# A three-layer macaron block on one core: each quad's maxima split on VectorE, side products in column tiles, another order of the plan

## The reference

```python
def ffn(x, W1, b1, W2, b2):
    h = relu(einsum('bsd,fd->bsf', x, quantize(W1)) + b1)      # 128 -> 512
    return einsum('bsf,df->bsd', h, quantize(W2)) + b2         # 512 -> 128
def attn(x, ...):                                              # 16 heads of 8
    q, k, v = (x @ W.T + b split into heads for W, b in ...)
    q, k = rope(q, k)
    scores = einsum('bhnd,bhmd->bhnm', q, k) / sqrt(8)
    return (softmax(scores) @ v).reshape(B, N, 128) @ Wo.T + bo
x = x + 0.5 * ffn(layernorm(x))
x = x + attn(layernorm(x))
x = x + 0.5 * ffn(layernorm(x))
```

## Time and profile before

| | |
|---|---|
| median of three runs | 545.3 us (545.23 to 552.78) |
| the profiled execution | 550.09 us, of it 548.3 us span on the core |
| granted TensorE clock, mean of the span | 0.975 |
| busy: TensorE, VectorE, ScalarE, GpSimd | 91%, 72%, 67%, 39% of the span |

### The profile page before, as it was taken

One profiled execution on the slowest core, in us unless ns is written; L12 is line 12 of the kernel. 1 busy time (PEld: TensorE's weight loads), 2 busy tenths in 40 slices (PEclk: granted clock), 3 DMA queues, 4 the chain that ended last, 5 costly groups with the idle time before them and its releaser, 6 DMA issues.

```text
span 548.3 us, 8622 instructions
## 1 busy us (share of the span) xinstructions
PE 501.3 (91%) x3197; PEld 233.6 (43%) x3197; DVE 393.3 (72%) x582; ACT 366.1 (67%) x440; POOL 213.7 (39%) x286
## 2 busy tenths in 40 slices
PE   6777897999999999999999998999899989998986
PEld 4554533433453435353535333533353434432445
DVE  5478575668887787768887788778877877887224
ACT  4667469586847675768666866687667757675751
POOL 3314356136455273447351555155514531103202
PEclk9998797999999999999999999999999989998999
DMA  8064036203350138003620345034502450000000
GB/s 275 4 207 100 1 91 197 62 1 118 115 118 3 41 131 195 5 22 116 177 57 3 115 136 119 1 97 151 123 2 80 163 127 2 22 2 2 3 19 20
DMA packets 18953, 44.21 MB, mean 81 GB/s; under 512 B 2400, under 2 KB 5472, under 8 KB 17888
## 3 DMA queue, kind: packets, MB, share of 16 engines
q1 hardware_dynamic: 18240, 43.14, 28.4%
q10 hardware_dynamic: 672, 0.52, 0.3%
HBM read 20.58 MB, written 18.87 MB: 72 GB/s over the span
## 4 chain that ended last, share of the span: by engine, by line
PE 67%; DVE 12%; ACT 10%; issue 5%; POOL 2%; POOLq 0%; ACTq 0%; DVEq 0%
PE heads_acc L563 21%; PE unit L548 12%; PE unit L533 11%; DVE maxima L863 8%; PE side L621 7%; ACT probs L758 5%; PE side L615 3%; PE side L609 3%; PE side L601 3%; PE side L587 2%; DVE x_lo L880 1%; ACT hidden L748 1%; ACT heads L764 1%; ACT x_hi L740 1%; PE side L582 1%
## 5 line engine op out<-in xcount | busy, mean ns | idle before, releaser
L863 DVE TENSOR_REDUCE maxima<-unit 128x2 f32<-128x1024 f32 x256 | 303.7, 1221 | 83.8 <-PE unit L533 82.0
L758 ACT ACTIVATE probs<-unit 128x1024 f32<-128x1024 f32 x256 | 254.6, 1024 | 105.0 <-PE unit L548 103.6
L563 PE MATMUL heads_acc<-probs,v_heads 128*32 128x512 f32 x1024 | 138.6, 615 | 1.1 <-ACT probs L758 1.1
L548 PE MATMUL unit<-q_stack,k_stack 64*128 64x512 f32 x512 | 114.5, 465 | 8.1 <-DVE maxima L863 4.5
L533 PE MATMUL unit<-k_stack,q_stack 62*128 62x512 f32 x512 | 107.4, 443 | 9.0 <-DVE maxima L863 4.5
L1052 POOL TENSOR_SCALAR max_parts<-maxima 128x16 fp32r<-128x16 f32 x32 | 6.5, 203 | 191.0 <-DVE maxima L863 190.9
L548 PEld LDWEIGHTS unit<-q_stack,k_stack 64*128 64x128 f32 x512 | 46.6, 185 | 75.6 <-DVE maxima L863 31.6
L533 PEld LDWEIGHTS unit<-k_stack,q_stack 62*128 62x128 f32 x512 | 47.8, 187 | 69.3 <-issue 30.1
L621 PE MATMUL side<-w_q,hidden 128*128 128x128 f32 x384 | 51.7, 288 | 0.8 <-ACT hidden L748 0.8
L621 PEld LDWEIGHTS side<-w_q,hidden 128*128 128x128 f32 x384 | 46.5, 197 | 11.2 <-issue 10.9
L748 ACT ACTIVATE hidden<-side,b_col 128x512 f32<-128x512 f32 x46 | 31.7, 690 | 12.5 <-PE side L615 12.5
(11 more groups left out here) (156 smaller groups left out, 483.6 us busy)
## 6 DMA issues: line engine op xcount, KB each, us to landing
k_scratch<-k_parts SPq DMA_DIRECT2D x16, 512.0 KB, 2.9
q_scratch<-q_parts SPq DMA_DIRECT2D x16, 512.0 KB, 3.5
k_stack<-k_scratch SPq DMA_DIRECT2D x14, 512.0 KB, 7.1
q_stack<-q_scratch SPq DMA_DIRECT2D x14, 512.0 KB, 9.0
resid<-in_x SPq DMA_DIRECT2D x8, 256.0 KB, 4.7
k_swap<-k SPq DMA_DIRECT2D x14, 128.0 KB, 2.3
q_swap<-q SPq DMA_DIRECT2D x14, 128.0 KB, 2.3
out_y<-resid SPq DMA_DIRECT2D x7, 256.0 KB, 2.1
```

What stands on the lines that cost most here:

```text
L548: mm = pe.matmul(to[:, e, :], k_stack[part, quad // NQ % 2, pair, kt * P:(kt + 1) * P], q_stack[part, quad // NQ % 2, pair, :], start=True ...
L563: mm = pe.matmul(heads_acc[32 * j:32 * j + 32, :], v_heads[:, b % 2, at, ODD * odd:ODD * odd + 32], probs[:, burst % RING, j, :], start=(k ...
L758: act.activation(probs[:, burst % RING, 2 * pp:2 * pp + 2, :], unit_of(USE_OF["exp", n]), ACT.Exp, scale=SCALE).then_inc(s_exp, 1)
L863: dve.tensor_reduce(maxima[:, quad % 2, :, r], unit_of(USE_OF["max", k]), AX_X, ALU.max).then_inc(s_max, 1)
```

## The change

Four things are changed.

1. `split_max` leaves GpSimd. VectorE does both of its operations in `max_of`, directly behind the eighth maximum of a quad.
2. q, k, v, `out`, `up` and `down` products of the plans are cut in four along the width of their stationary operand (`COLUMNS`), each quarter in its own column tile, with a quarter of the output partitions. In the opening they stay whole (`WHOLE`).
3. VectorE's order in the opening: q's second part goes ahead of v; the statistics and the normalisation of batch 3 go between the first maxima, and the statistics of batch 4 behind the `LEAD` loop; the side parts beside the maxima come one maximum later. ScalarE makes q's first part earlier. More fills, and other banks and places for batch 3's feed-forward layer and the first `max_T`.
4. Both plans are written anew.

```diff
-FILL = {("attn_T", 0, 0): 16, ("k", 0, 0): 3}
+FILL = {("ffn1_up", 0, 0): 6, ("attn_T", 0, 0): 38, ("k", 0, 0): 3, ("ffn1_T", 0, 2): 8, ("ffn1_up", 0, 2): 8}
...
                 elif name.endswith("_down"):
                     if arg == 0:
                         pe.wait_ge(s_hid[which], (index + 1) * FT)
                     for n in range(FT):
-                        mm = pe.matmul(to[:, arg * P:(arg + 1) * P], hidden[:, n, arg * P:(arg + 1) * P],
-                                       w2_q[:, n, :], start=(n == 0), stop=(n == FT - 1))
+                        for cols in tiles:
+                            mm = pe.matmul(to[cols, arg * P:(arg + 1) * P],
+                                           hidden[:, n, arg * P + cols.start:arg * P + cols.stop],
+                                           w2_q[:, n, :], start=(n == 0), stop=(n == FT - 1))
...
+                wait(dve, s_var[n], j * T)
                 for t in range(T):
                     dve.bn_stats(stats[n][:, t, :], resid[:, j * T + t, :]).then_inc(s_stats[n], 1)
...
                 dve.tensor_reduce(maxima[:, quad % 2, :, r], unit_of(USE_OF["max", k]), AX_X, ALU.max).then_inc(s_max, 1)
+                if r == QSTEPS - 1:
+                    whole = maxima[:, quad % 2, :, :]
+                    wait(dve, s_maxT_psum, quad)
+                    dve.wait_ge(s_max, k + 1)
+                    dve.tensor_scalar(max_parts[:, :, 0, :], whole, 1.0, 0.0, ALU.mult, ALU.add).then_inc(s_split, 1)
+                    dve.wait_ge(s_split, quad * SPLIT_STEPS + 1)
+                    dve.tensor_tensor(max_parts[:, :, 1, :], whole, max_parts[:, :, 0, :].bitcast(F32),
+                                      ALU.subtract).then_inc(s_split, 1)
...
             rotate_sum("q")
+            second_part("q")
             dve.wait_ge(s_v_fill, 2)
             dve.wait_ge(s_bv, 1)
             side_part(("v", 0, 0, 5))
-            second_part("q")
             open_ln("ffn1", 2)
             side_part(("ffn1_down", T - 1, 1, 6))
             side_part(("ffn1_T", 0, 2, 1))
             ln_stats("attn", 1)
-            open_ln("ffn1", 3)
-            ln_stats("ffn1", 4)
             for k in range(LEAD):
                 max_of(k)
-                for use in BESIDE_MAX.get(k, ()):
+                if k == 0:
+                    ln_stats("ffn1", 3)
+                if k == 2:
+                    ln_apply(dve, "ffn1", 3)
+                for use in BESIDE_MAX.get(k - 1, ()):
                     side_part(use)
+            side_part(BESIDE_MAX[LEAD - 1][-1])
+            ln_stats("ffn1", 4)
```

The other products are cut like `down`. The new plans begin so, the first line of each being the one that the prediction speaks of (`PE_FIRST`, then `PE_STEADY`):

```diff
-e m m attn_T@1
-e k@1
+attn_T@1 ffn1_stats@5 e
+e m k@1 m
...
-ffn1_T m e
-heads_copy1@-1 m pv ffn1_up0 e m ffn1_up1
+m ffn1_T e m pv
+heads_copy1@-1 ffn1_up0 e m ffn1_up1
+e m heads_T1@-1
```

More of the change, by code:

```diff
@@ L45 @@
 SPLIT_STEPS = 2
+COLUMNS = [slice(32 * c, 32 * c + 32) for c in range(4)]
+WHOLE = [slice(0, P)]
 FIRST_CONST_DMAS = 4
@@ L614, in side_work @@
                     for n, part in enumerate((x_hi, x_lo)):
-                        mm = pe.matmul(to, w1_q[:, arg * P:(arg + 1) * P], part[:], start=(n == 0), stop=(n == 1))
+                        for cols in tiles:
+                            mm = pe.matmul(to[cols, :], w1_q[:, arg * P + cols.start:arg * P + cols.stop], part[:],
+                                           start=(n == 0), stop=(n == 1))
                     mm.then_inc(s_up[which], 1)
```

134 lines of the change are left out of this document (59 added, 75 removed).

## The result

The change makes the kernel slower: 567.8 us (566.5 to 570.6) beside 548.1 in the same series, a ratio of 1.037 with a 95% interval of 1.029 to 1.044. The forecast was 534, with a range of 525 to 543. The ratios here leave out disturbed executions, the medians hold all, so that a ratio is not always the quotient of two medians.

A forecast was written before the change was run, and what follows sets the result against it. The prediction saw an opening of chained waits, a plan 0 with gaps and seven plans led by TensorE. Plans 1 to 7 (−6.5) and opening with plan 0 (−5.0) gave −11.5 from 545.3: 534 us, range 525 to 543.

The forecast's parts named there:

- Tiles, −6.3: Side products of all plans: column tiles and abutting bursts save 6.3 us in all, 5.6 of it in plans 1 to 7.
- More instructions ... cost nothing as long as four tiles run at once: Tiled side products: four times as many instructions add no time, as bursts were taken to show.
- second rival: Side products: tiles give nothing, rounds being set by something else than columns; 540 us, chance 0.11.
- fifth rival: `down`, v and out products: tile loads don't hide beside the matmuls, costing 37 us; 571 us, chance 0.06.
- `ffn2_T`, −5.9: Plans 1 to 7, before `ffn2_up0`: seven TensorE waits of 0.84 us go, covered by a burst and three more units.
- New short covers, +1.0: Plans, before `ffn1_up1` and `out`: only two units cover ScalarE's evacuation, 0.3 us per plan, some 1.0 us in all.
- The split, +4.0: VectorE, plans 1 to 7: 28 splits of 0.45 us, a third on the path, cost 4.0 us (bounds 0 and 12.6).
- Opening, −0.3 to −3.2: Opening: earlier first scores and maximum let the last `down` end at 63.1 to 66.0 us, before 66.35.
- first rival: Opening: it gives nothing, the wait for GpSimd and a clock fall eating the earlier start; 539 us, chance 0.18.
- If the clock falls in the stall, VectorE's queue covers most of it: Head of plan 0: a slow clock behind TensorE's stop was expected to cost little; no separate size given.
- with 3 to 6 us of waits: Plan 0: TensorE's waits in the stretch after VectorE's pacing; plan 1 starts 63 to 66 us behind the last `down`.
- Opening and plan 0 together: Opening and plan 0: combined gain of 2 to 8 us, taken as 5.0.

The follow-up runs named there:

- g6_heads_behind: Kernel before with, in the later plans, `ffn2_T` ahead of a unit and a burst and `heads_copy0` behind that burst; 544.7 us, 0.998.
- o1_opening_alone: Kernel before with the new opening alone; plans, split and whole-array products as before; 547.7 us, 1.003.
- g1_mended_whole: Changed kernel with `ffn1_stats@5` late, `max_T3` of plan 0 and `max_T1` of later plans earlier, an `up` moved, all side products whole; 546.1 us, 0.995.
- g4_mended_gpsimd: As g1_mended_whole, but with the split on GpSimd again, at its places in the kernel before; 540.4 us, 0.986.
- e1_max_early: Changed kernel with `max_T2` of the later plans moved ahead by two score units, one exponential's unit and one burst; 566.5 us, 1.024.
- g5_one_word: Kernel before with one word of the later plans moved, `ffn2_T` ahead of a score unit and a burst; 564.5 us, 1.027.

## Why the prediction was wrong

The sign was wrong. Of the parts, alone on the kernel before, tiles cost 4.3 us, the split 8.3, the opening 1.5 and the plans 0.4 (ratios times 546), which add up to 14.5. In company they cost 20. The difference lies within the intervals; what the traces show only in company is the stop at the head of plan 0.

1. *Tiles, −6.3.* The prices were right (1.01, 0.88 for 0.85, 0.54 for 0.55). The step that failed is "More instructions ... cost nothing as long as four tiles run at once": it looked at the array and its weight loads, not at where instructions come from, and so put that price at nothing: alone the tiles made the kernel 4.3 us slower, where −4 to −6 was expected of them on the plans of before. There is one stop of 4.35 us in the change, there are two of 4.79 and 3.19 with the tiles alone, each with a slow clock behind it. The second rival (tiles give nothing) had the direction but not the mechanism, and its price of 540 was far off. Near in number is the fifth rival (571), but its mechanism is excluded: the loads of the tiles are hidden, or `down` would not take 1.01. The rule that stands beside the second rival, of the Trainium skill's TensorEngine Tiling (Array Packing), section "When to Use Tiling", is not what happened either: a `down` block, 128 wide, in four tiles did gain 0.08 us. (By the rounded prices shown, the eight `up` come to +0.08 and not +0.12, and an abutment saves 0.13 and not 0.14; the sum stays near −1 us a plan.) On code, the Trainium skill says in Runtime: NRT & Kernel Launch, section "Instruction fetch mechanics", that an engine's code comes in blocks of 16 KiB over a DMA queue of its own and that the cost is mostly hidden. The trace agrees on the blocks (26 and 40 of 16 KB) and on most of them being hidden; it differs where they meet the loads of a batch, where 11 of 47 ended a stop of 0.8 to 5.4 us. The trace has no record of when a block was asked for, so that its wait behind the loads is inferred and not shown: from the 1.3 to 1.7 us between a block's landing and TensorE's going on, from whole products having no such stop, and from the stops' end in the two kernels with tiles and spaced loads, where a few words of the plans had moved too.

2. *`ffn2_T`, −5.9.* The waits went, all seven (in the order a burst and four units stand there now, not three); the gain measured alone is 0.9 us. The step "Now a burst and three more units lie between ...: −5.9" credited a wait of the leading engine in full. In plan 2 of `g6_heads_behind` TensorE gains those 0.84 us and loses 0.58 of them again within 2 us, where it meets ScalarE's pace. In the other plans this was not followed.

3. *New short covers, +1.0.* The two named, in front of `ffn1_up1` and `out`, measure 0.18 us and nothing; instead `ffn1_up2` waits 0.74, 0.75 and 0.47 us in plans 1 to 3, for VectorE's `attn_out`. That is some 2.5 us for the forecast's 1.0, at another place. Missed was the cover that mattered, a term put at nothing. In plan 4 the rows of quad 1, which stand on SyncE ahead of q's scratch and the loads, go out 10.1 us into the plan (before 7.7), so that the loads are later, while the unit that needs the rows of quad 2 is due sooner; the rows wait behind the loads, 10.3 us of stops in plans 4 to 6. In plans 1 to 3, with `ffn1` between, the rows come 9.5 us behind the loads (165.96 − 156.44), and nothing waits. In the kernel before, plan 4's loads go out at 326.32 and its rows at 332.67, without a stop but with little to spare: `o1_opening_alone`, with the same plans, has one such stop of 0.80 us. The prediction never asked what stands ahead of a moved step on SyncE's queue.

4. *The split, +4.0.* Size: some 8 alone, and 5.7 between `g1_mended_whole` and `g4_mended_gpsimd`; both within the bounds of 0 and 12.6. The 0.45 us each was right; "a third" on the path was too little: 1.6 of 1.8 us in plan 1 of the split alone, about half by the last pair. VectorE was busy for 46.6 of 59.5 us; that its free time was not where the quads end is the likely reason, and was not followed.

5. *Opening, −0.3 to −3.2.* Nothing, as the first rival said. Plan 0's first exponential starts between 66.1 and 70.8 us in six traces with the old opening and between 65.1 and 71.2 in thirteen with the new one (means 68.6 and 68.4).

6. *Plan 0.* The stop was forecast as 3.7 us with VectorE waiting 4; it was 3.78 and 3.81. The clock behind it read 0.56, 0.50 and 0.80 for 9 us, and yet taking the stop away shortened the plan up to its eighth exponential by 3.8 us (up to its fifth by 6.2), no more than the stop's own length: "If the clock falls in the stall, VectorE's queue covers most of it" is borne out here. What failed is "with 3 to 6 us of waits": TensorE's waits over 0.15 us in plan 0 are 12.4 us (3.78, the 4.35 of the code, 1.27 for rows of maxima, and shorter ones), and plan 1 starts at 140.1 us, 75 behind the last `down` (64.9) and not 63 to 66. Opening and plan 0 together were forecast as −5.0 and came to +6.1.

The clock runs through all of this. By the span's means it lost (1 − 0.961) × 565.1 = 22 us of full speed in the changed kernel and (1 − 0.975) × 548.3 = 14 before, so that up to 8 of the 20 us are TensorE at the lower level, most of it behind the stops.

## What to carry to other kernels

A reordering is checked against the transfer queues as well as the engines: for each DMA that something waits for, ask what stands ahead of it on its queue, and how much margin it had before. Unrolling one wide operation into four narrow ones has a second price besides the engine's, the code, which shares the DMA engines with the data; large loads in spaced pieces seem to leave room for both. The change became 2.9% faster instead of 3.7% slower only by several steps together: the loads in two halves with the rows between them, the split back on GpSimd, whole `up` products and a few words of the plans moved. A stop of TensorE can cost more than its length, because the clock falls behind it (6.8 us for 4.79 with the tiles alone, but 3.8 for 3.78 at the head of plan 0), and a wait that is removed pays in full only where the other engines had the time to use it.

## What the runs showed of the hardware

TensorE can stop for 0.8 to 5.4 us (5.35 in `e1_max_early`), some of the times in the middle of a product, where no semaphore stands; each time a 16 KB block of instructions lands 1.3 to 1.7 us before it goes on, behind loads that kept the DMA engines at a share of about 1. That the late block is the cause is inferred. Two small DMAs behind four loads of 512 KB on one queue reach their reader 8.0 us after issue in place of 3.4, and it makes no difference whether they are issued 4.25 or 5.4 us behind the first load (13.01 and 13.08 us from that load to the reader). Moving a single word of a plan cost 2.7% (`g5_one_word`): ScalarE, which takes its work in order, stood at the heads, the wait before the `up` grew by 0.51 us, and the clock fell to 0.50 behind three of the waits; these don't add up to the whole 15 us, and the rest was not followed.
